# Moving the next pair's layer-norm statistics, the row transposes and the last products in an attention pipeline

## The reference

```
h = tok(x)                       # x: 32 x 4 x 250; two recurrences of 8 steps -> h: 32 x 250 x 64
h = h + attn(layernorm(h))       # 8 heads, scores = exp(-gamma * |q - k|^2), no softmax
h = h + ffn(layernorm(h))        # 16 experts, the best 2 of each token, then a layer norm

def attn(x):
    xn = ln(x, ln_scale)
    Q, K, V = xn @ W_q[h], xn @ W_k[h], xn @ W_v[h]          # per head h, 64 x 64 each
    q2, k2 = sum(Q*Q), sum(K*K)                              # per token and head
    scores = exp(-gamma * max(q2 + k2 - 2 Q K^T, 0))         # 250 x 250 per head and batch row
    return concat_h(scores @ V) @ W_o.T
```

## Time and profile before

| | us |
|---|---|
| median of 3 runs | 790.02 (790.01 to 790.14) |
| profiled execution | 790.59 |
| its span in the trace | 788.7 |
| PE busy | 733.5 (93%) |
| DVE / ACT / POOL busy | 567.0 / 484.8 / 452.0 |
| granted TensorE clock, mean | 0.994 of full speed |

### The profile page before, as it was taken

How to read it: one execution, slowest core, us unless ns; L and a number is a source line. 1 busy time by engine, 2 the same in 40 slices (tenths; PEclk the granted TensorE clock), 3 DMA queues, 4 the chain that set the end, 5 groups by cost and what they waited for, 6 DMA issues and landing times.

```text
span 788.7 us, 17033 instructions
## 1 busy us (share of the span) xinstructions
PE 733.5 (93%) x5712; PEld 438.5 (56%) x5712; DVE 567.0 (72%) x1474; ACT 484.8 (61%) x993; POOL 452.0 (57%) x620
## 2 busy tenths in 40 slices
PE   2999989999999999999999999899999999999994
PEld 1343346667666766667666776544455555544441
DVE  7576766676666757666666765688888888888874
ACT  1466767677676867768676777555555555554541
POOL 7644314644456443654446423256878878788785
PEclk9999999999999999999999999999999999999998
DMA  6300214465555745465445655000000000000000
GB/s 184 94 2 2 54 40 97 104 158 122 116 115 124 159 111 119 103 144 136 111 112 119 158 123 117 1 2 1 9 8 14 9 9 8 8 12 11 9 7 20
DMA packets 41821, 56.22 MB, mean 71 GB/s; under 512 B 16360, under 2 KB 40680, under 8 KB 41608
## 3 DMA queue, kind: packets, MB, share of 16 engines
q1 hardware_dynamic: 40744, 53.87, 29.7%
q10 hardware_dynamic: 992, 1.26, 0.6%
HBM read 5.06 MB, written 2.43 MB: 9 GB/s over the span
## 4 chain that ended last, share of the span: by engine, by line
PE 54%; DVE 13%; POOL 13%; issue 9%; ACT 8%; DMA 2%; ACTq 0%; POOLq 0%; DVEq 0%
PE bank L1454 13%; PE bank L1432 13%; PE bank L1193 5%; ACT prob L673 5%; POOL sq L483 5%; PE bank L1280 4%; DVE prob L958 3%; PE bank L1349 3%; PE bank L1351 3%; DVE qk L900 3%; PE bank L1322 2%; POOL inv L450 2%; POOL inv L458 2%; ACT cs L629 2%; PE bank L1183 2%
## 5 line engine op out<-in xcount | busy, mean ns | idle before, releaser
L958 DVE TENSOR_SCALAR prob<-prob,cap_hi,cap_lo 125x500 f32<-125x500 f32 x256 | 136.3, 550 | 54.3 <-ACT prob L673 54.3
L673 ACT ACTIVATE prob<-bank 125x500 f32<-125x500 f32 x256 | 154.3, 630 | 4.4 <-PE bank L1351 4.3
L1432 PE MATMUL bank<-cs,w_sb 64*64 64x500 f32 x1024 | 147.0, 580 | 2.2 <-DVE gated L1077 2.0
L1454 PE MATMUL bank<-gated,w_sb 64*64 64x500 f32 x1024 | 148.7, 588 | 0.0
L527 POOL TENSOR_TENSOR gated<-relu,wb 128x500 f32<-128x500 f32 x96 | 120.0, 1252 | 50.0 <-ACT relu L773 47.5
L1077 DVE SCALAR_TENSOR_TENSOR gated<-bank,nb,wb 128x500 f32<-128x500 f32 x160 | 114.9, 727 | 37.1 <-PE bank L1432 37.1
L483 POOL TENSOR_TENSOR sq<-sq 125x256 f32<-125x256 f32 x128 | 99.4, 792 | 66.2 <-DVE qk L900 43.4
L773 ACT ACTIVATE relu<-bank,b_sb 128x500 f32<-128x500 f32 x96 | 64.7, 674 | 93.7 <-PE bank L1432 93.7
L637 ACT ACTIVATE sq<-bank 125x512 f32<-125x512 f32 x128 | 75.7, 610 | 19.8 <-POOL sq L483 19.6
L448 POOL TENSOR_TENSOR inv<-aggr,eps 125x4 f32<-125x4 f32 x16 | 3.2, 201 | 146.7 <-DVE aggr L881 146.7
L1432 PEld LDWEIGHTS bank<-cs,w_sb 64*64 64x64 f32 x1024 | 53.1, 133 | 54.7 <-issue 48.1
(11 more groups left out here) (188 smaller groups left out, 1560.1 us busy)
## 6 DMA issues: line engine op xcount, KB each, us to landing
m1o<-cs SPq DMA_DIRECT2D x128, 125.0 KB, 2.4
m<-mlow SPq DMA_DIRECT2D x120, 125.0 KB, 2.3
m1e<-cs SPq DMA_DIRECT2D x112, 125.0 KB, 2.4
out<-res SPq DMA_DIRECT2D x15, 125.0 KB
w_sb<-in_w SPq DMA_DIRECT2D x1, 1024.0 KB
m1e<-m1e SPq DMA_DIRECT2D x8, 125.0 KB, 2.3
xa<-xparts SPq DMA_DIRECT2D x3, 281.2 KB
w_sb<-in_w SPq DMA_DIRECT2D x1, 512.0 KB
```

What stands on the lines that cost most here:

```text
L673: act.activation(prob[(8 * (p - 1) + v) % PROBS][:, :, c, :], bank[5 + n % 3][0:T, 0:C].rearrange("p (h l) -> p h l", h=2), ACT.Exp).then_ ...
L958: dve.tensor_scalar(part, part, cap_hi[0:T, h:h + 1], cap_lo[0:T, h:h + 1], ALU.min, ALU.max)\
L1432: last = pe.matmul(up_bank(g)[cols, 0:C], w1_sb[rows, g, cols], cs1[q % 3][rows, :], start=True, stop=True)
L1454: last = pe.matmul(y[cols, 0:C], w2_sb[rows, g, :], gated[g % 8][rows, :], start=v == 0, stop=v == 7, skip_group_check=True)
```

## The change

Four edits, all of them moves; no instruction is added or dropped.

1. DVE: `norm_stats(p + 1)` and `norm_aggr(p + 1)` go from the end of slot 0 to the head of the step, ahead of `stack_b(p)` and of the two clamps of slot 0.
2. PE: `rows_b(p)` goes from the end of slot 4 into slot 5, behind `scores(5, 0)` and unit 9.
3. ACT: `round_rows(p)` goes to the same place, behind `Exp` of `scores(5, 0)` and unit 9; with that it also falls behind `evac_y(p - 1, 0)`.
4. PE: in step 16 the products of slots 4 and 5 of the last pair go from the tail (step 17) to the end of slot 6, ahead of `start_c(6)`.

```
@@ ScalarE, step_b
                         rest = rest[1:]
+                        if new and v == 5 and c == 0:
+                            round_rows(p)
                     for k in rest:
                         unit(p, j, k, unit_bank(k))
-                    if new and v == 4:
-                        round_rows(p)
                     if v == 4 and old:
                         evac_y(p - 1, 0)
@@ VectorE, step_b
+                if ln:
+                    norm_stats(p + 1, b_ln)
+                    norm_aggr(p + 1, b_ln)
                 for v in range(8):
                     if new and v == 0 and not first_step(p):
                         stack_b(p, j)
...
-                    if ln and v == 0:
-                        norm_stats(p + 1, b_ln)
-                        norm_aggr(p + 1, b_ln)
@@ TensorE, step_b
                         if rest:
                             unit(rest.pop(0))
+                        if new and v == 5 and c == 0:
+                            rows_b(p)
                     for k in rest:
                         unit(k)
+                    if v == 6 and p == PAIRS:
+                        for n in (4, 5):
+                            for hh in range(2):
+                                products(p - 1, n, o, hh)
...
-                    if new and v == 4:
-                        rows_b(p)
@@ TensorE, step_b_tail
                 if p == PAIRS + 1:
-                    for n in range(4, 8):
+                    for n in (6, 7):
```

## The result

The changed kernel took **764.8 us** (median of 4 runs, 764.06 to 765.8) against 790.08 us (790.01 to 791.52, 4 runs) for the kernel before: a ratio of 0.9677, interval 0.966 to 0.9694. The forecast was 766.0, range 764 to 770.5. In a later comparison, the run **after_again**, it took 766.32 us against 791.38, ratio 0.9682 (0.9667 to 0.9697). The profiled execution took 765.8 us, with a span of 764.0.

A forecast was written before the change was run, and what follows sets the result against it. PE's own stream, busy 93% of the span, was taken as the bound. 19.0 + 0.94 + 2.4 + 1.65 = 24.0 us off the profiled 790.59 gives 766.6, less 0.57 for the median: 766.0, range 764 to 770.5.

The forecast's parts named there:

- The changed step: Steps 2 to 14: period from 25.16 to 23.7 us, 1.46 less per step, 19.0 in all; bounds 0.94 and 1.55.
- PE is free at T+12.19: Ordinary step, T being unit 8's start on PE: products start at T+8.67, sixteen take 3.52, then PE is free.
- The prediction's 0.94 for the order alone: Ordinary step: if the chain did not shorten, the moved score and unit give 1.02 - 0.08 = 0.94 us.
- Rival (b): Behind the row transposes: ACT becomes the bound, a third of a microsecond per step stays, 770.3 us; chance 0.12.
- `stack_b`, priced at nothing: DVE, ordinary step: `stack_b` ends some 0.7 us later, at about 238.3; unit 8 needs it at 240.05, so no cost.
- Rival (d): Ordinary step: `stack_b` comes too late and unit 8 waits, at most 0.7 us a step, 775.1 us; chance 0.04.
- Step 1, 2.4 forecast: Step 1: statistics 1.45 us earlier, PE's stall from 2.50 to about 1.05, gain 2.4; 1.4 if the clock falls.
- rival (c): POOL's norm chain slows beside DVE's work, 3.7 us if each operation waits for one DVE instruction; 793.9 us, chance 0.03.
- The trace agrees that they don't block: Step 1 before the change: POOL's chain beside DVE's clamps took 4.67 us against 4.56, so 0.1, not 3.7.
- 1.05 is nearest to the first, so I take it that it stays up: Step 1 clock: stays up after stalls up to 1.4 us, fell after 2.50; at about 1.05 it should stay up.
- The end of stage B, 1.65 forecast: Half the sixteen products fill PE's 2.54 us stall before the weight transposes: 1.65 us sooner, bounds 0 and 1.76.
- Step 15, 0.94 forecast: Step 15 has no norm chain; transposes stay, the score and unit move into the wait: 0.94 us.

The follow-up runs named there:

- stats_only: Kernel before plus only the norm statistics moved to the head of the step on DVE; row transposes and rounding not moved: 782.82 us, ratio 0.989.
- act_rows_early: Changed kernel with ACT's rounding of the rows put back at the end of slot 4, PE's row transposes still in slot 5: 780.46 us, ratio 0.9862.
- rows_two_later: Changed kernel with row transposes and rounding one more score and unit later, behind scores(5,1) and unit 12, on PE and ACT: 777.62 us, ratio 0.9826.
- step1_early_stats: Changed kernel with the statistics of pair 2 moved further up, ahead of stack_b(1, 1), which stands before step 1: 762.47 us, ratio 0.9642.
- both_ends: Changed kernel with pair 2's statistics before stack_b(1,1), ACT's second normed one slot later, and slot 6's products ahead of the weight transposes: 762.45 us, ratio 0.9634.
- tail_only: Kernel before plus only the last pair's products of slots 4 and 5 moved ahead of the weight transposes: 788.32 us, ratio 0.9958.

## Why the prediction was right

**The bound.** PE's own stream sets the time, and the gain is its removed idle time: right. PE makes up 88% of the chain that ended last, and 54% before.

**The changed step, 1.46 forecast, 1.54 measured.** The row transposes come at T+13.12; the sum had 13.08 by the chain and 13.21 by PE. The step of the working that was off is "PE is free at T+12.19", a number of the kernel before: there the products start at T+8.67, and without POOL's norm chain in the way of the squares they start at T+8.48, as **stats_only** shows by itself. PE is ready 0.2 us sooner, so it is the chain's 13.1 that counts, and the 0.08 for a slow start after the transposes did not show. 13.12 + 5.09 + 5.43 = 23.64. The better bound, 1.55, was the right one.

**What the two edits do.** The shorter chain and the fill of the wait were priced as if they met; they do, and each one's share is now known: 0.515 and 1.02. The prediction's 0.94 for the order alone was 0.08 low.

**ACT, edit 3.** The prediction told it as a gain that goes with the move. It is the condition of it: without it, 1.0 us a step is lost again (**act_rows_early**). Rival (b), ACT as the bound, has its mechanism in that kernel; in the changed one ACT itself waits 59.5 us for PE's products, and PE for ACT almost nowhere after step 1.

**`stack_b`, priced at nothing.** Right: unit 8 never waits for it; the 2.9 us of cover held. Rival (d) did not happen.

**Step 1, 2.4 forecast, 1.91 measured; with a falling clock 1.4 forecast, 0.48 measured (29.08 - 28.60).** Two steps failed. First, the statistics did come 1.5 us sooner, but the chain behind them grew from 4.67 to 5.32 us (111.31 to 116.63), so PE's stop fell to 1.63 + 0.26 and not to 1.05. This is rival (c)'s mechanism, at a fifth of its price here and at a twentieth (0.18 of 3.7 us) in an ordinary step. The rows of the changed kernel, DVE, POOL and PE:

```profile
111.31 0.60 DVE L873 BATCH_NORM_STATS2 stats<-h_all 125x6 f32<-125x64 f32 x4
116.63 1.40 POOL L483 TENSOR_TENSOR sq<-sq 125x256 f32<-125x256 f32 x2
118.09 0.50 PE L1280 MATMUL bank<-wqku_hi,s 128*125 128x512 f32 x1 [1.63 <-ACT sq L637]
```

POOL's timeline in step 1 before:

```profile
114.19 0.20 POOL L448 TENSOR_TENSOR inv<-aggr,eps 125x4 f32<-125x4 f32 x1 [23.00 <-DVE aggr L881]
114.47 1.14 POOL L450 TENSOR_TENSOR inv<-inv,mhalf 125x4 f32<-125x4 f32 x1
115.69 0.20 POOL L452 TENSOR_TENSOR inv<-aggr,inv 125x4 f32<-125x4 f32 x1
```

and after, POOL and then DVE:

```profile
112.41 0.40 POOL L448 TENSOR_TENSOR inv<-aggr,eps 125x4 f32<-125x4 f32 x1 [21.47 <-DVE aggr L881]
112.89 1.39 POOL L450 TENSOR_TENSOR inv<-inv,mhalf 125x4 f32<-125x4 f32 x1
114.36 0.39 POOL L452 TENSOR_TENSOR inv<-aggr,inv 125x4 f32<-125x4 f32 x1
...
112.25 0.96 DVE L958 TENSOR_SCALAR prob<-prob,cap_hi,cap_lo 125x500 f32<-125x500 f32 x2
113.71 0.98 DVE L958 TENSOR_SCALAR prob<-prob,cap_hi,cap_lo 125x500 f32<-125x500 f32 x2
```

Add start and duration. L448 ends at 112.81, and of the pair of clamps that started at 112.25 (0.51 each by the trace) the first ends 0.05 earlier. L450 starts inside the second, which ends at 113.21; 0.05 later and with its 1.02 it ends at 114.28. That is also 0.04 after the end, at 114.24, of the first of the next two clamps, so this row alone doesn't tell which of the two held it; the first is the likelier, since that later clamp had begun only 0.20 us before L450 would have ended, and an L450 of **rows_two_later** that meets a clamp so late (0.21) is not held. L452 ends at 114.75, the pair from 113.71 at 114.69. Where DVE has no clamp in flight, L454 to L460 take their old 0.20 and 1.01. In an ordinary step it is L450 alone: it would end at 230.35, inside the pair of clamps that ends at 230.48, and ends at 230.53. Over the whole trace of the changed kernel, of the 112 operations of the norm chain 16 have a clamp in flight at their undisturbed end, and all 16 end 0.04 to 0.06 us after that clamp; the other 96 are never more than 0.02 us longer than their kind. Over all 13 profiles 173 operations are held, each until 0.04 to 0.06 us after a clamp. Five are not held although a clamp is in flight at their end (L452 and L458 in **step1_early_stats** and **both_ends**, one L450 in **rows_two_later**); in these five the clamp had begun only 0.11 to 0.21 us before. `stack_b`, which reads a PSUM bank, lengthens nothing: L448 runs beside it with 0.20 at 229.05.

So POOL is held by the clamps. The prediction said of the Trainium skill's rule in "SBUF — State Buffer", section "Who interferes with whom": "The trace agrees that they don't block". That was misread. What the rule says, that the two engines share ports and one blocks the other for a whole instruction in a two-port mode, fits what the traces show, though none shows which mode the clamps run in and no run took the clamps away. Even the kernel before had the sign: L450's 1.14 in place of 1.02 ends at 115.61, 0.04 after the two clamps that start at 114.59. What was wrong in rival (c) was only the price. An operation doesn't wait for a whole clamp each time but for the rest of the one in flight, 0.18 to 0.37 us, and only where they meet: three times in step 1 (0.20 + 0.37 + 0.19 = 0.76, less the 0.12 that was there before: 0.64 of the 0.65), once in an ordinary step, where POOL's slack of 1.37 us covers it. (c) needed 3.2 us.

Second, "1.05 is nearest to the first, so I take it that it stays up" was a guess between 1.4 and 2.50 without a row in between. At the real 1.6 it stays up in five profiles of seven, so that it stayed up in the first profile was in part luck. The other branch was mis-sized too: the forecast put a fall at 2.4 - 1.4 = 1.0 us, and it costs 1.43.

**The end of stage B, 1.65 forecast, 1.68 measured** (**tail_only**), and the wait of PE 0.57 instead of 0.8 to 1.0. The weight transposes come 40.19 us after the T of step 15 with and without the edit; what is won is the half of the products that no longer stands behind them, 1.84 us instead of 3.52. **Step 15, 0.94 forecast**: T to the first score of the next batch 19.24 before, 18.28 after, 0.96.

**The sum.** 24.0 forecast, 24.5 by the marks: +1.0 in the ordinary steps, -0.5 in step 1. The two misses are opposite in sign, so the total is better than its terms, and that is luck. The median came 1.2 us below the forecast of 766.0. Of these 0.5 is in the marks; 0.26 is the earlier first score; the other 0.4 is that the profiled execution lies 1.0 us above its median and not the 0.57 that was carried over.

## What to carry over

When an engine at 93% waits in every step for a chain through three others, look for two things at once: what of its own next work can be put ahead of the wait, and what stands ahead of the chain on the engines that carry it. Here they gave 1.02 and 0.52 us an ordinary step and added up. Move the waiting instruction on the engine that consumes the result as well, or that engine's queue becomes the next wait; and find the slack of whatever comes after the moved step, since half a slot more cost 0.7 us a step.

Judge such a change from landmarks on the busiest engine (first score, T, first instruction of the next stage), not from medians alone: of two kernels that differ by 1 us, the start of a stage may vary by more.

## What was not expected of the hardware

GpSimd operations of 0.20 us were held to the end of a VectorE clamp of 0.51 us that was in flight, and took up to 0.41; a power of 1.02 took up to 1.39. In **step1_early_stats** it is other operations of the same chain (L454, L456 and L460 with 0.41, 0.37 and 0.38) that meet the clamps. So on these two engines the position of an instruction of 0.2 us relative to the other's clamps decides what it costs, and moving a chain to an earlier place can put it beside busier neighbours.

The granted TensorE clock can differ between two executions of the same program at the same place: after a stop of 1.6 us it stayed at 1.00 in five profiles and fell to 0.5 for 3.41 us in two. With a stop of 2.5 us in step 1 it fell every time, yet after the one of 2.54 us at the end of stage B it did not the earlier trace rows. A gain that rests on the clock staying up is not safe until the stop itself is gone, as in **step1_early_stats**.
